# A windowed softmax: the maximum as bias of 16 small exponentials, their sums gathered on the way

## The reference

```python
def attn_layer(x, Wqkv, qs, ksc, Wo):
    q, k, v = jnp.split(x @ Wqkv, 3, -1)            # 16 heads x 64
    q, k = l2norm(q) * qs, l2norm(k) * ksc
    ...                                             # rotary positions with a scale
    sim = jnp.einsum('bhwie,bhwje->bhwij', bq, bk2) * 8.0
    sim = jnp.where(mask, -jnp.finfo(sim.dtype).max, sim)
    attn = jax.nn.softmax(sim, -1)                  # over 64 keys
    out = jnp.einsum('bhwij,bhwje->bhwie', attn, bv2)
    ...
    return out @ Wo

def ffn_layer(x, g, bln, W1, b1, W2, b2):
    xn = (x - mu) / jnp.sqrt(var + 1e-05) * g + bln
    a, gate = jnp.split(xn @ W1 + b1, 2, -1)
    return a * jax.nn.gelu(gate, approximate=False) @ W2 + b2
```

## Time and profile before

| | |
|---|---|
| median of three runs | 3166.56 us (3165.83 to 3168.74) |
| the profiled execution's own time | 3168.24 us |
| its span, first to last instruction | 3166.5 us |
| TensorE busy (PE) | 3005.7 us, 95% |
| VectorE busy (DVE) | 2880.3 us, 91% |
| ScalarE busy (ACT) | 2272.7 us, 72% |
| GpSimd busy (POOL) | 1807.9 us, 57% |
| mean granted TensorE clock | 0.99 of full |
| HBM traffic | 27 GB/s over the span |

### The profile page before, as it was taken

The page is one execution under the profiler, slowest core; times in us unless marked ns, Lnnn a source line. Parts: engine busy times, 40 slices in busy tenths (PEclk is TensorE's granted clock), DMA queues, the critical chain, the costliest instruction groups (busy, mean ns, idle before and its releaser), DMA issues.

```text
span 3166.5 us, 93664 instructions
## 1 busy us (share of the span) xinstructions
PE 3005.7 (95%) x37896; PEld 1857.5 (59%) x37896; DVE 2880.3 (91%) x2671; ACT 2272.7 (72%) x3707; POOL 1807.9 (57%) x823
## 2 busy tenths in 40 slices
PE   8699999999999999999999999999999999999996
PEld 4356555665665566565566656556656555665653
DVE  5599999999999999999999999999999999999995
ACT  4467777777777777776667777777777777777774
POOL 8556565555656555555445565555656565555652
PEclk9799999999999999999999999999999999999998
DMA  9544544543544544454344354454445445445542
GB/s 317 169 110 116 144 115 107 145 122 98 156 117 101 144 117 117 118 154 113 84 133 106 91 152 117 107 133 124 112 121 141 112 122 133 112 118 134 125 112 59
DMA packets 254405, 398.04 MB, mean 126 GB/s; under 512 B 51148, under 2 KB 84872, under 8 KB 254280
## 3 DMA queue, kind: packets, MB, share of 16 engines
q1 hardware_dynamic: 254280, 396.41, 47.8%
HBM read 64.64 MB, written 19.92 MB: 27 GB/s over the span
## 4 chain that ended last, share of the span: by engine, by line
PE 40%; DVE 23%; ACT 19%; issue 10%; SPq 1%; POOL 1%; DMA 1%; DVEq 0%; ACTq 0%; POOLq 0%
PE ps L848 6%; PE ps L806 5%; PE ps L866 5%; PE ps L882 5%; PE ps L827 5%; PE ps L787 4%; ACT f_ab L1094 4%; DVE f_mx L1362 4%; DVE f_p L1365 3%; ACT f_u L1093 3%; DVE f_p L1377 3%; ACT ps L1105 3%; PE ps L789 3%; PE ps L788 3%; ACT f_p L1111 3%
## 5 line engine op out<-in xcount | busy, mean ns | idle before, releaser
L1291 POOL TENSOR_TENSOR f_w<-f_w,f_ab 128x1024 f32<-128x1024 f32 x192 | 549.2, 2861 | 526.9 <-DVE f_w L1342 526.9
L1296 POOL TENSOR_TENSOR f_ab<-f_w,f_rn 128x1024 f32<-128x1024 f32 x192 | 594.1, 3094 | 390.9 <-DVE f_rn L1352 380.9
L1287 POOL TENSOR_TENSOR f_u<-f_u 128x512 f32<-128x512 f32 x384 | 589.1, 1549 | 365.3 <-ACT f_u L1093 359.8
L1094 ACT ACTIVATE f_ab<-ps,f_pa 128x512 f32<-128x512 f32 x768 | 542.1, 706 | 1.2
L1093 ACT ACTIVATE f_u<-ps 128x512 f32<-128x512 f32 x768 | 467.1, 608 | 99.3 <-PE ps L789 93.6
L1342 DVE TENSOR_TENSOR f_w<-f_ab,f_tan 128x1024 f32<-128x1024 f32 x384 | 500.4, 1343 | 4.1 <-POOL f_ab L1296 2.3
L848 PEld LDWEIGHTS ps<-f_tb,f_v 128*64 128x64 f32 x6144 | 396.0, 137 | 102.1 <-issue 78.5
L848 PE MATMUL ps<-f_tb,f_v 128*64 128x160 f32 (+1 forms) x6144 | 442.2, 297 | 11.9 <-DMA f_tb<-f_pt 10.7
L1105 ACT ACTIVATE ps<-ps 128x512 f32<-128x512 f32 x384 | 204.7, 574 | 340.7 <-PE ps L806 340.2
L787 PE MATMUL ps<-f_xh,f_wh 128*128 128x512 f32 x768 | 380.7, 496 | 54.8 <-ACT f_ab L1094 44.5
L806 PE MATMUL ps<-f_u,f_ones 128*128 128x512 f32 x768 | 370.2, 604 | 6.9 <-POOL f_u L1287 4.1
(11 more groups left out here) (165 smaller groups left out, 4822.9 us busy)
## 6 DMA issues: line engine op xcount, KB each, us to landing
f_kb<-f_ab SPq DMA_DIRECT2D x384, 256.0 KB, 3.6
f_qb<-f_ab SPq DMA_DIRECT2D x384, 256.0 KB, 3.6
f_tb<-f_pt SPq DMA_DIRECT2D x1344, 64.0 KB
f_wh<-split_w SPq DMA_DIRECT2D x48, 384.0 KB, 4.4
f_wl<-split_w SPq DMA_DIRECT2D x48, 384.0 KB, 4.2
a_w_raw<-wqkv SPq DMA_DIRECT2D x24, 384.0 KB, 4.6
split_w<-a_w_hi SPq DMA_DIRECT2D x24, 384.0 KB, 4.6
split_w<-a_w_lo SPq DMA_DIRECT2D x24, 384.0 KB, 5.5
```

The costliest lines, as they stand in the source:

```text
L1094: nc.scalar.activation(ab[:, g % 2, i, :], bank("qk", g, i), ACT.Identity, scale=pa[:, g, i:i + 1]).then_inc(qk_read.sem, 1)
L1287: nc.gpsimd.tensor_tensor(u[:, 2 * i + 1, :], u[:, 2 * i, :], u[:, 2 * i + 1, :], ALU.add).then_inc(sq_sum[i].sem, 1)
L1291: nc.gpsimd.tensor_tensor(w[:, 0:2, :], w[:, 0:2, :], ab[:, k % 2, 0:2, :], ALU.add).then_inc(q_sum.sem, 1)
L1296: nc.gpsimd.tensor_tensor(ab[:, k % 2, 0:2, :], w[:, 0:2, :], rn[:, 0:1, :].broadcast_to([128, 2, N]), ALU.mult).then_inc(rope_q.sem, 1)
```

## The change

Three things are done differently. The maximum is written with its sign turned (`negate=True`), and the subtraction is gone. In its place ScalarE runs 16 exponentials a quad, one for each row of 64 scores in PSUM, with that row's negated maximum as bias (a [128, 1] pointer) and with `accum_out`, which gathers the sum of the 64 results into a column of `rs`; so VectorE's sum is gone too, and only the reciprocal is left in `sums`. With the subtraction goes its semaphore: `mask_scores` now waits for `p_exp`, the signal of the 16th exponential, and ScalarE takes over the wait for the transpose of the quad before (`p_tr`), since it is now the first to write `p`. And in VectorE's list rotations (`turn`, `add_keys`) or other pieces stand between a maximum and its inverse. The lists of TensorE, ScalarE, GpSimd and SyncE keep their order.

```diff
-        s_max, s_sub, p_exp = per_quad("s_max"), per_quad("s_sub", ahead=1), per_quad("p_exp")
-        p_sum, p_inv, p_norm = per_quad("p_sum"), per_quad("p_inv"), per_quad("p_norm")
+        s_max, p_exp = per_quad("s_max"), per_quad("p_exp", ahead=1)
+        p_inv, p_norm = per_quad("p_inv"), per_quad("p_norm")
...
+                srow, rows_of = ps[:, SS[0]:SS[1] + 1, :].rearrange("p a (n k) -> p (a n) k", k=2 * WIN), pb.rearrange("p b n k -> p n b k")
...
                         def mask_scores(g):
 
-                            pe.wait_ge(s_sub.sem, now.count(s_sub, g - 1))
+                            pe.wait_ge(p_exp.sem, now.count(p_exp, g - 1))
...
                         def exponentials(g):
-                            act.wait_ge(s_sub.sem, now.count(s_sub, g))
-                            nc.scalar.activation(p[:, :], p[:, :], ACT.Exp).then_inc(p_exp.sem, 1)
+                            act.wait_ge(s_max.sem, now.count(s_max, g))
+                            act.wait_ge(p_tr.sem, now.count(p_tr, g - 1))
+
+                            for n in range(16):
+                                last = nc.scalar.activation(rows_of[:, n], srow[:, n].rearrange("p (b k) -> p b k", b=2), ACT.Exp,
+                                                            bias=mx[:, n:n + 1], accum_out=rs[:, n:n + 1])
+                            last.then_inc(p_exp.sem, 1)
...
                             dve.wait_ge(s_ready.sem, now.count(s_ready, g))
-                            nc.vector.tensor_reduce(mx[:, :], srow, AX.X, ALU.max).then_inc(s_max.sem, 1)
-                            dve.wait_ge(s_max.sem, now.count(s_max, g))
-                            dve.wait_ge(p_tr.sem, now.count(p_tr, g - 1))
-                            nc.vector.tensor_tensor(rows_of, srow.rearrange("p n (b k) -> p n b k", b=2),
-                                                    mx[:, :].unsqueeze(2).unsqueeze(3).broadcast_to([128, 16, 2, WIN]), ALU.subtract).then_inc(s_sub.sem, 1)
+                            nc.vector.tensor_reduce(mx[:, :], srow, AX.X, ALU.max, negate=True).then_inc(s_max.sem, 1)
 
                         def sums(g):
 
                             dve.wait_ge(p_exp.sem, now.count(p_exp, g))
-                            nc.vector.tensor_reduce(rs[:, :], rows_of, AX.XY, ALU.add).then_inc(p_sum.sem, 1)
-                            dve.wait_ge(p_sum.sem, now.count(p_sum, g))
                             nc.vector.reciprocal(rs[:, :], rs[:, :]).then_inc(p_inv.sem, 1)
...
                             normalise_keys(0)
                         if prev:
                             less_maximum(-1)
+                        if cur:
+                            turn(1)
+                            add_keys(1)
+                        if prev:
                             sums(-1)
-                        if cur:
-                            turn(1)
-                        if prev:
                             turn_weights(-1)
                         if cur:
-                            add_keys(1)
                             normalise_keys(1)
                             less_maximum(0)
+                            turn(2)
+                            add_keys(2)
                             sums(0)
                             turn_weights(0)
                         if prev:
                             residual()
-                        if cur:
-                            turn(2)
-                            add_keys(2)
-                        if prev:
                             centred()
...
                             turn(3)
+                            evacuate_out()
                             sums(1)
-                            evacuate_out()
                             turn_weights(1)
...
                             normalise_keys(3)
-                            sums(2)
                         if prev:
                             second_residual()
...
                         if cur:
+                            sums(2)
                             turn_weights(2)
```

More of the change, by code:

```diff
@@ L485, in build_hybrid @@
         RET_READ = dict(var="lnv", k="k_part", kr="kr_part", qr="qr_part", v="v_sb", q="q_part", s0="g0", s1="g1", s2="g2", out="x2", mean2="xc2", var2="lnv2")
-        GRANTED = [xs_done, x_hi, x_lo, n_ready, rope_q, rope_k, k_dma, q_dma, s_ready, s_sub, p_tr, t_dma, *o_ready, *o_read, x2, val_done]
+        GRANTED = [xs_done, x_hi, x_lo, n_ready, rope_q, rope_k, k_dma, q_dma, s_ready, p_exp, p_tr, t_dma, *o_ready, *o_read, x2, val_done]
         SP_USES = [*((1, c) for c in range(-1, 3)), *((4, c) for c in range(-2, 2)), (8, -4), (8, 0)]
@@ L491, in build_hybrid @@
                     *((128, c) for c in range(-64, 33, 32)), *((512, c) for c in range(-640, -255, 128))]
-        ACT_USES = [(1, -1), (3, -5), (3, -4), (3, -3), *((4, c) for c in range(-3, 2)), *((8, c) for c in range(-7, 1)),
+        ACT_USES = [(1, -1), (3, -5), (3, -4), (3, -3), *((4, c) for c in range(-4, 2)), *((8, c) for c in range(-7, 1)),
                     *((16, c) for c in range(-15, 1)), (32, 32), *((128, c) for c in range(-96, 1, 32))]
@@ L1332, in bank @@
                             return bank_of(order, *which)
-                        f, rows_of = ps[:, FB, :], pb.rearrange("p b n k -> p n b k")
+                        f = ps[:, FB, :]
                         def turn(k):
@@ L1526, in step @@
                             less_maximum(-1)
-                            sums(-1)
                         if cur:
                             turn(1)
+                            add_keys(1)
                         if prev:
+                            sums(-1)
                             turn_weights(-1)
                         if cur:
-                            add_keys(1)
                             normalise_keys(1)
                             less_maximum(0)
+                            turn(2)
+                            add_keys(2)
                             sums(0)
```

1 line of the change is left out of this document (removed).

## The result

The changed kernel takes 4112.15 us (median of four runs, 4109.21 to 4113.58) against 3167.17 us before: a ratio of 1.298, 95% interval 1.296 to 1.3005. It is slower by 945 us. That lies within the range given, near its upper end, and 289 us above the likeliest time. An ordinary step went from 61.3 to 81.9 us in the mean (42 of them make 865 us), a retention step from 72 to about 89 us.

The account below looks back on a forecast made before the run. TensorE was taken as the bound, busy 59.52 of a 61.34 us step. Added waits and clock, 601 + 50 + 4 = 655 us over 3168.24 us, gave 3823 us (chance 0.48), range 3500 to 4150 us.

Parts of the forecast that it names:

- VectorE's relief: Subtraction and sum leave VectorE, 9.8 us a step; at most 1.82 us a step could come back, none was counted.
- The block: A quad's 16 exponentials on ScalarE: 0.288 us each, 4.6 us together, 3.63 us more than the single exponential.
- Nothing overlaps: Rival: each sum is taken after its activation has run out, 6.8 us per 16 exponentials; 4366 us, chance 0.14.
- the sum is free: Rival: gathering sums costs nothing, 3.0 us per 16 exponentials; 3430 us, up to 3480 with the clock, chance 0.14.
- a): Step boundary: quad 2's exponentials stand behind quad 3's inverse norms, delaying TensorE's mask matmul; 4.1 us added.
- b): Quad -1: value and output copies come behind the exponentials, delaying norms and the fourth value projection; 2.5 us added.
- c): Quad 0: the output copy comes behind the exponentials, and the output projection needs it; 1.0 us added.
- d): Quad 1: the scaling comes behind the exponentials, and six hidden matmuls need it; 3.65 us added.
- The clock: TensorE returns at 1.2 GHz after half of waits a) and d), 3.0 us each; 3.0 us a step charged.
- the sentence on the moved rotations: Rotations between maximum and inverse only fill VectorE's time; nothing on SyncE's queue or GpSimd waits earlier; no cost counted.
- The sum: All added time: 601 us for 42 ordinary steps, 50 us for five retention steps, 4 us at the end: 655 us.
- the signs of being wrong: TensorE's waits for exponentials under 100 us, ScalarE filling the step without waiting, or spacing far from 0.29 us.

Follow-up runs that it names:

- experiment 7: The changed kernel without accum_out, VectorE summing again before the inverse: 3821.2 us, ratio 1.2066.
- 8: The changed kernel with 8 exponentials a quad, each over two rows with one maximum and one sum for both: 3728.8 us, ratio 1.1774.
- experiment 6: The kernel before, keeping its subtraction and VectorE order, with 16 exponentials a quad that gather sums without bias: 3637.5 us, ratio 1.1487.
- 9: The kernel of experiment 1 with each first mask matmul moved to right before its scores: 3957.3 us, ratio 1.2489.
- 10: The kernel of experiment 1 with quad 1's exponentials behind the scaling and last value copies, and quad 2's mask matmul right before its scores: 3966.3 us, ratio 1.2525.
- experiment 1: The changed kernel with quad 2's rotation and its addition put back behind the residual in VectorE's list: 3892.2 us, ratio 1.2294.
- experiment 5: The kernel of experiment 1 with constant matmuls filling TensorE's two long waits, at the step's start and before quad 2's mask matmul: 3766.7 us, ratio 1.1882.
- experiment 3: The changed kernel with VectorE's whole old order, including quad 1's rotation and the sums: 3891.6 us, ratio 1.2284.
- experiment 4: The changed kernel with 12 constant matmuls an ordinary step filling three of TensorE's waits: 3971.0 us, ratio 1.2539.

## Why the prediction was right or wrong, point by point

- **VectorE's relief is worth nothing.** Right as far as the runs show. VectorE fell to 60% of the span, and TensorE's largest waits all end with ScalarE, though the one before the mean only passes on a wait of VectorE. Waits for the transfer of late softmax weights add 35 us, in seven places.
- **The block.** Right to 2%: 0.29 us apart, 4.7 us. The price of the sum (0.09 us: 0.29 with it, 0.20 without, in experiment 7) came out as that of one more operand, a guess that happened to fit: the sum is an instruction of its own. "Nothing overlaps" and "the sum is free" fall.
- **a) to d).** a) 4.1 was 4.1 (4.37 less the 0.26 before), b) 2.5 was 2.2, c) 1.0 was 0.7, d) 3.65 was 3.4: 11.3 expected, 10.4 measured. Experiments 7 and 8 show for a, b and d that they follow the block one for one, 6, 9 and 10 that it is the place in ScalarE's list that costs, not the held banks.
- **The clock.** This term of the sum was too small. It had 3.0 us a step, for waits a and d alone. In the changed kernel the same matmuls take 6.2 us more a step: the clock also falls behind b and behind the mean's wait. With the rotation put back, a step is 15.5 us longer than before, and the waits a to d make some 10.4 of it, so about 5 us are left for the clock, and it still falls behind b (0.50 from 1193.00 to 1196.00 in experiment 1). That experiment 5 returns just 3.0 us a step with fillers at a and d alone fits the number, not the account of it, since the clock then also falls less often behind b. The rule of the Trainium skill that was weighed there (TensorE: Matmul & The Clock Gate, section HAM oscillation — how this bites in real kernels) would have had the clock fall at each wait. The trace agrees for four of the five waits of a step, and not for the shortest, c (0.66 us), behind which the clock is 1.00.
- **The step that failed** is the sentence on the moved rotations: they "only fill VectorE's time while ScalarE works", and "nothing on SyncE's queue or GpSimd's waits earlier for them". Nothing waits earlier, but the rotation of quad 2 itself waits, for GpSimd's normalised queries, and the inverse, the product, the transpose and the residual are queued behind it. By the prediction's own rule for an added wait this had to be priced: in the step of the trace before, the maximum of quad 0 ended at 1062.8, and quad 1's queries were normalised on GpSimd from 1065.1 to 1067.4. It costs 220 us in the changed kernel (experiment 1), 5.1 us a step. The rotation of quad 1 fails the same sentence in the retention steps (experiment 3): 17 us longer each, where 10 were taken, against 10 to 12 with the old order.
- **The sum.** With VectorE's whole old order (experiment 3) the change costs 724 us, where the sum had 655: an ordinary step is some 16 us longer, where it had 14.3, and all the others make some 50 us, where it had 54. That rest of 69 us is in the main the clock. The remaining 220 of the 289 us are the order.
- **The range.** That 4112 us lie inside it is luck. Its upper end stood for a block of 5.9 us, and the block was 4.7; without the moved rotations the time would have been 3892, 2% above the likeliest, for the reasons given.
- **What was to be seen after:** VectorE near 2410 us (2475), ScalarE near 2960 (2991), spacing 0.29 (0.29), a step of 75 to 76 us (81.9), a clock visibly below 0.99 (0.904). None of the signs of being wrong that it named came up: the waits for exponentials total 386 us, ScalarE has idle time, the spacing fits. They watched the block, and none of them watched VectorE's order.

## What to carry to other kernels

An instruction cut into sixteen holds its in-order queue sixteen fixed costs long (here 4.7 us, where the single one held it for 1.0). Before moving work to an engine with idle time, list what stands behind the new block in that engine's queue and who waits for it, since a share of 72% busy says nothing of that. A piece put in front of another to fill a gap brings its own waits along: price them as you would an added wait, and look first for a tile that another engine still reads. And where the matmul engine begins to wait several times a step, its lower clock comes on top: here 6.2 us a step, with four waits of 2.2 to 4.7 us behind which it fell.

## What the runs showed of the hardware that was not expected

- A gathered sum is an instruction of its own behind each activation, 0.09 us of pace (0.20 to 0.29 us), though its row is 0.2 to 0.3 us long. A bias by pointer, and PSUM in place of SBUF as the source, together add 0.05 us to short neighbours (0.24 in experiment 6, 0.29 in the changed kernel); the two were not told apart.
- Work added to TensorE's idle time made the kernel faster, twice: by 141 us (12 matmuls a step, experiment 4) and by 125 us (7, experiment 5).
- VectorE's product of the weights (L1378) took 3.13 us at 1450.73, and 1.23 us where GpSimd was idle; in the mean 1752 ns against 1514 before. At 1450.73 GpSimd was adding the queries it had just been given. Of all 192 such products in the profile after, the 101 beside which GpSimd does nothing take 1.22 us in the mean, the 49 that it overlaps in part 3.12 us, and the 42 that it overlaps from end to end 1.42 us. That the two hinder each other fits, by an amount that depends on what GpSimd does; it was not tested.
